# Bilinear samplers of a deformable convolution: samples from plain source tiles, weighted afterwards

## The reference

```python
off1 = conv2d(x, w_off1, b_off1, stride=1, pad=1)          # 18 planes: 9 taps x (dy, dx)
out  = relu(bn_inf(deform_conv(x, off1, w_dc1, 1, 2, 2), g1, beta1, m1, v1))
off2 = conv2d(out, w_off2, b_off2, stride=1, pad=1)
out  = bn_inf(deform_conv(out, off2, w_dc2, 1, 2, 2), g2, beta2, m2, v2)
return relu(out + x)
# deform_conv: for each tap (ky, kx) and each place (y, x) of the output
#   ys = y - 2 + 2*ky + dy ; xs = x - 2 + 2*kx + dx        (pad 2, dilation 2)
#   sampled[i, tap, y, x] = bilinear sample of image channel i at (ys, xs), zero outside
#   out[o, y, x] = sum over i and tap of weight[o, i, tap] * sampled[i, tap, y, x]
```

## Time and profile before

| | |
|---|---|
| median of 3 runs | 812.22 us (811.79 to 814.93) |
| the profiled execution: time, span | 817.21 us, 815.4 us |
| mean granted TensorE clock | 0.840 |
| TensorE matmul / weight load busy | 676.4 us (83%) / 499.2 us (61%), 17818 each |
| VectorE / ScalarE / GpSimd busy | 444.7 us (55%) / 413.7 us (51%) / 132.7 us (16%) |
| DMA | 16.37 MB, of which queue "instruction" 1.98 MB in 121 packets |

### The profile page before, as it was taken

One profiled execution on the slowest core, in us unless ns is written; L12 is line 12 of the kernel. 1 busy time (PEld: TensorE's weight loads), 2 busy tenths in 40 slices (PEclk: granted clock), 3 DMA queues, 4 the chain that ended last, 5 costly groups with the idle time before them and its releaser, 6 DMA issues.

```text
span 815.4 us, 38530 instructions
## 1 busy us (share of the span) xinstructions
PE 676.4 (83%) x17818; PEld 499.2 (61%) x17818; DVE 444.7 (55%) x797; ACT 413.7 (51%) x819; POOL 132.7 (16%) x215
## 2 busy tenths in 40 slices
PE   6788888888858788988778648899999999996556
PEld 1356666666633466665666546688888888874344
DVE  0575555554714555566456482456666666675543
ACT  0667555654414766556455042445666655554512
POOL 7000000000021000000000023324433334420400
PEclk8979797996769798788877665589999999998768
DMA  6400000000002200000000063000000000000002
GB/s 186 86 7 4 5 4 4 4 5 4 5 6 54 37 5 4 4 5 4 5 4 5 4 134 105 2 2 1 0 0 0 0 0 0 0 1 1 1 1 104
DMA packets 7677, 16.37 MB, mean 20 GB/s; under 512 B 1837, under 2 KB 5805, under 8 KB 7141
## 3 DMA queue, kind: packets, MB, share of 16 engines
q1 hardware_dynamic: 7534, 14.21, 7.2%
HBM read 10.34 MB, written 3.87 MB: 17 GB/s over the span
## 4 chain that ended last, share of the span: by engine, by line
PE 75%; issue 9%; ACT 7%; DVE 7%; DMA 1%; POOL 1%; SPq 0%; DVEq 0%; ACTq 0%
PE banks L228 20%; PE banks L145 14%; PE banks L717 8%; PE banks L761 5%; PE banks L694 5%; PE banks L742 4%; PE banks L459 4%; PE banks L776 4%; PE banks L181 2%; ACT hx L274 2%; PE banks L167 2%; PE banks L707 1%; DVE norm_stats L630 1%; ACT y L484 1%; DMA src<-in_x_dram 1%
## 5 line engine op out<-in xcount | busy, mean ns | idle before, releaser
L319 DVE TENSOR_TENSOR s<-hy,hx 128x384 f32<-128x384 f32 (+3 forms) x336 | 144.5, 476 | 147.9 <-PE banks L228 145.9
L228 PE MATMUL banks<-s,y 32*64 32x96 f32 (+9 forms) x10752 | 182.9, 262 | 50.9 <-issue 50.7
L228 PEld LDWEIGHTS banks<-s,y 32*64 32x64 f32 x10752 | 154.6, 149 | 91.2 <-issue 81.5
L145 PE MATMUL banks<-w_dc,tiled 64*64 64x192 f32 x1792 | 121.4, 409 | 13.1 <-issue 7.3
L269 ACT COPY y<-banks 128x384 f32<-128x384 f32 x192 | 80.9, 487 | 95.3 <-PE banks L145 95.3
L145 PEld LDWEIGHTS banks<-w_dc,tiled 64*64 64x64 f32 x1792 | 78.0, 166 | 36.3 <-issue 14.1
L279 ACT ACTIVATE hy<-banks 128x512 f32<-128x512 f32 (+2 forms) x144 | 73.3, 582 | 32.1 <-PE banks L181 31.8
L880 DVE TENSOR_REDUCE stats<-banks 128x16 f32<-128x1024 f32 x32 | 39.2, 1225 | 72.8 <-PE banks L717 72.8
L958 POOL TENSOR_TENSOR y<-y,stats 128x1024 f32<-128x1024 f32 x32 | 60.8, 1901 | 108.2 <-DVE stats L890 108.1
L274 ACT ACTIVATE hx<-banks 128x384 f32<-128x384 f32 x144 | 61.2, 504 | 23.9 <-PE banks L167 19.6
L717 PEld LDWEIGHTS banks<-src,y 64*128 64x128 f32 x1024 | 66.2, 205 | 8.1 <-issue 8.1
(11 more groups left out here) (134 smaller groups left out, 742.5 us busy)
## 6 DMA issues: line engine op xcount, KB each, us to landing
src<-in_x_dram SPq DMA_DIRECT2D x4, 578.0 KB, 5.7
y<-in_w_dram SPq DMA_DIRECT2D x1, 2080.0 KB
off<-in_w_dram SPq DMA_DIRECT2D x2, 1024.0 KB
out_dram<-tokens SPq DMA_DIRECT2D x4, 512.0 KB, 2.6
offsets_dram<-tokens SPq DMA_DIRECT2D x32, 54.0 KB
off<-offsets_dram SPq DMA_DIRECT2D x16, 108.0 KB
w_dc<-in_w_dc_dram SPq DMA_DIRECT2D x2, 288.0 KB, 6.7
y<-in_w_attn_dram SPq DMA_DIRECT2D x1, 512.0 KB, 4.8
```

The costliest lines, as they stand in the source:

```text
L145: last = nc.tensor.matmul(m.ps[C * half:C * half + C, FIRST_BANK + (count + g) % RING, (col % 2) * 192:(col % 2) * 192 + 192], m.tiled[row ...
L228: last = nc.tensor.matmul(out[:, r0:r0 + strip.n, first:first + width], m.y[32 * j:32 * j + 32, g, (s // 3) % 2 * Y_SLOTS + strip.slot, co ...
L319: nc.vector.tensor_tensor(dst, hy, hx[:, :, r0:r0 + strip.n, :], ALU.mult).then_inc(cv.s_ready, 1)
```

## The change

The order of the two products in a sampler is turned round: first plain pixels are sampled, for three kernel columns at once, then the samples are weighted.

- The work is cut into 24 units (4 output rows, ky). A unit has 2 or 3 strips, one for each row of tiles that can reach it: two of 4 rows for ky 0 and 2, one of 4 and two of 2 rows for ky 1, fewer at the image's borders. `sample` makes 32 products per strip; each has 3 x rows x 12 columns (144 or 72) and isn't clipped. Its weights are pixels themselves, from `xt`, the source with pixels on partitions. The banks 0 to 3 hold one unit's samples (3 kernel columns x 4 rows at a pitch of 40).
- At the end of a unit ScalarE takes the samples of two pairs of images, and VectorE those of the other two (`take`, 768 elements each), to `sampled`. The next unit's sampling waits for both.
- When three units have made the 9 taps of 4 rows, `final_pe` weights them: items ("f", row, k) of 9 x 2 x 2 products on 64 x 64 tiles, 128 columns long. ScalarE finishes them (`finish0`, `finish1`). In the second convolution w_dc is scaled by batch norm on VectorE beforehand, and x is added by four products with the identity per item.
- `xt` for the first convolution is laid out on the host and loaded, 2.1 MB, on SP's queue ahead of the loads of w_dc, sel and places. For the second, GpSimd stages the finished rows (`stage_pool`, 4 copies), TensorE turns them (`turn_pe`, items ("t", row), 16 products), and ScalarE copies them to `xt`.
- Coordinates: two items of columns per unit (8 products each, bf16) and one or two of rows (2 products per strip); ScalarE evicts an item of both groups in one activation. The plan puts the items of the unit after next between the groups of 8 sampling products or behind the unit.
- The products of hats for group g = 0 stay on VectorE, those for g = 1 go to GpSimd (`weigh`), one instruction of 12 x rows x 12 elements (576 or 288) per strip and engine. VectorE makes the hats of both groups in one instruction per kind.
- `tiles_pool`, the weighted products and the first weighted items in `offsets_pe` and `offsets_act` go. ScalarE now takes a square root of a loaded row ahead of its first eviction, and for that waits for the loads of the first convolution.

```diff
-IMAGES = [[0, 2, 1, 3], [5, 7, 4, 6]]
+IMAGES = [[0, 2, 4, 6], [1, 3, 5, 7]]
 ROW_COORD, ROW_ONE, ROWS_OFF = 12, 13, 14
-RING, FIRST_BANK = 4, 4
-Y_SLOTS = 5
+FIRST_BANK = 4
+
+UNIT_ROWS = TILE_ROWS
+PLACES = UNIT_ROWS * W
+UNITS = [(row, ky) for row in range(H // UNIT_ROWS) for ky in range(3)]
+PITCH = W + WIN_COLS - TILE_COLS + REACH + 2
+HAT_PITCH = W + 2
+HAT_ROW = 3 * HAT_PITCH
+X_HATS, Y_HATS = 3 * TC * UNIT_ROWS * WIN_COLS, 2 * UNIT_ROWS * HAT_ROW
...
+class Unit:
+    def __init__(self, u, strips_before):
+        self.u = u
+        self.row, self.ky = UNITS[u]
+        self.strips = []
+        for tile_row in range(TR):
+            first = TILE_ROWS * tile_row - 2 * self.ky - UNIT_ROWS * self.row
+            last = min(first + WIN_ROWS, UNIT_ROWS)
+            first = max(first, 0)
+            if last > first:
+                self.strips.append(Strip(tile_row, first, last - first))
+        self.before = strips_before
...
+class Plan:
...
+        self.items = self.units[0].coords + self.units[1].coords
+        self.first = len(self.items)
+        for unit in self.units:
+            row, ky = UNITS[unit.u]
+            todo = self.units[unit.u + 2].coords if unit.u + 2 < len(UNITS) else []
+            final = [("f", row - 1, ky)] if row and ky < 2 else []
+            turn = [("t", row - 2)] if turns and row >= 2 and ky == 2 else []
+            cut = len(todo) if final else (len(todo) + 1) // 2
+            unit.inside, unit.behind = todo[:cut], todo[cut:] + final + turn
+            if unit.u == len(UNITS) - 1:
+                unit.behind = unit.behind + [("f", row, 0), ("f", row, 1)]
+                if turns:
+                    unit.behind = unit.behind + [("t", row - 1), ("t", row)]
+            self.items = self.items + unit.inside + unit.behind
...
-def weighted_pe(nc, pe, m, cv, count, tile_row, part, ky):
...
+def columns_pe(nc, m, cv, bank, u, part):
+
+    row, ky = UNITS[u]
+    kx, n = (0, 2) if part == 0 else (2, 1)
+    for c in range(TC):
         for g in range(2):
             rows = group_rows(g, 1)
+            at = offset_at(row, 3 * ky + kx, 0) + TILE_COLS * c - 2 * kx
+            last = nc.tensor.matmul(
+                ap(m.ps[:, bank + g, c * UNIT_ROWS * WIN_COLS:], [[X_HATS // 3, n], [WIN_COLS, UNIT_ROWS], [1, WIN_COLS]]),
+                m.sel[rows, c, :], ap(m.off_flat[rows, at:], [[HALF_PIX - 2, n], [W, UNIT_ROWS], [1, WIN_COLS]]),
+                start=True, stop=True, skip_group_check=True)
+    last.then_inc(cv.filled, 1)
...
+            last = nc.tensor.matmul(
+                ap(m.ps[:, bank + g, 3 * W * (strip.at % UNIT_ROWS):], [[W, 3], [3 * W, strip.n], [1, W]]),
+                m.sel[rows, strip.tile_row, :], ap(m.off_flat[rows, at:], [[HALF_PIX, 3], [W, strip.n], [1, W]]),
+                start=True, stop=True, skip_group_check=True)
...
+def final_pe(nc, m, cv, bank, row, k):
+
+    for tap in range(TAPS):
+        for p in (k, k + 2):
+            for g in range(2):
+                half = half_of(p, g)
+                rows = slice(C * half, C * half + C)
+                last = nc.tensor.matmul(m.ps[C * g:C * g + C, bank + p // 2, 0:PLACES], cv.w_dc[rows, tap, :],
+                                        m.sampled[rows, row % 2, p, tap, :], start=(tap == 0),
+                                        stop=(tap == TAPS - 1 and cv.k == 0), skip_group_check=True)
+    if cv.k:
+        for p in (k, k + 2):
+            for g in range(2):
+                rows = source_half(m.convs[0], p, g)
+                last = nc.tensor.matmul(
+                    m.ps[C * g:C * g + C, bank + p // 2, 0:PLACES].rearrange("p (r c) -> p r c", c=W),
+                    m.identity[rows, rows], image_rows(m.convs[0].src, p, row)[rows, :, :], start=False, stop=True,
+                    skip_group_check=True)
+    last.then_inc(cv.filled, 1)
...
+def turn_pe(nc, m, bank, tile_row):
+    for c in range(TC):
+        for j in range(PAIRS):
+            last = nc.tensor.matmul(m.ps[32 * j:32 * j + 32, bank, c * P:(c + 1) * P], m.stage[:, tile_row % 2, j, c, :],
+                                    m.identity[:, :], start=True, stop=True, skip_group_check=True)
+    return last
...
+    def sample(unit, strip, c):
+        n = strip.count
+        if c == 0:
+            for g in range(2):
+                pe.wait_ge(cv.s_ready[g], n + 1)
+        for j in range(PAIRS):
+            for g in range(2):
+                half = half_of(j, g)
+                out = m.ps[C * half:C * half + C, j, strip.first * PITCH + TILE_COLS * c + 4:]
+                places = strip.n * WIN_COLS
+                last = nc.tensor.matmul(
+                    ap(out, [[UNIT_ROWS * PITCH - 2, 3], [PITCH, strip.n], [1, WIN_COLS]]),
+                    m.xt[32 * j:32 * j + 32, strip.tile_row, c, C * g:C * g + C],
+                    ap(m.s[32 * j:32 * j + 32, n % SLOTS, g, c * places:], [[TC * places, 3], [WIN_COLS, strip.n], [1, WIN_COLS]]),
+                    start=(strip is unit.strips[0] and c == 0), stop=True, skip_group_check=True)
+        if c == TC - 1:
+            last.then_inc(cv.sampled, 1)
...
+    for unit in cv.plan.units:
+        groups = [(strip, c) for strip in unit.strips for c in range(TC)]
+        if unit.u:
+            for taker in range(2):
+                pe.wait_ge(cv.taken[taker], unit.u)
+        started = 0
+        for k, (strip, c) in enumerate(groups):
+            sample(unit, strip, c)
+            while started < len(unit.inside) and started * len(groups) < len(unit.inside) * k:
+                item_pe(n)
+                n += 1
+                started += 1
+        for _ in unit.inside[started:] + unit.behind:
+            item_pe(n)
+            n += 1
...
+def take(copy, m, cv, unit, j):
+
+    return copy(ap(m.sampled[:, unit.row % 2, j, 3 * unit.ky, :], [[TAPS * PLACES, 2], [W, 3 * UNIT_ROWS], [1, W]]),
+                ap(m.ps[:, j, 4:], [[BANK, 2], [PITCH, 3 * UNIT_ROWS], [1, W]]))
+
+
+def take_waits(engine, cv, unit):
+    engine.wait_ge(cv.sampled, unit.before + len(unit.strips))
+    if unit.row >= 2 and unit.ky == 0:
+        engine.wait_ge(cv.filled, cv.plan.items.index(("f", unit.row - 2, 1)) + 1)
+
+
+def weigh(multiply, engine, m, cv, unit, strip, g):
+
+    n = strip.count
+    if n >= SLOTS:
+        engine.wait_ge(cv.sampled, n - SLOTS + 1)
+    if strip is unit.strips[0]:
+        engine.wait_ge(cv.hats, 2 * unit.u + 2)
+    hy = ap(m.hy[:, unit.u % 2, g, strip.at * HAT_ROW:], [[TILE_COLS, 3 * TC], [HAT_ROW, strip.n], [1, WIN_COLS]])
+    hx = ap(m.hx[:, unit.u % 2, g, strip.first * WIN_COLS:],
+            [[UNIT_ROWS * WIN_COLS, 3 * TC], [WIN_COLS, strip.n], [1, WIN_COLS]])
+    dst = ap(m.s[:, n % SLOTS, g, :], [[strip.n * WIN_COLS, 3 * TC], [WIN_COLS, strip.n], [1, WIN_COLS]])
+    multiply(dst, hy, hx, ALU.mult).then_inc(cv.s_ready[g], 1)
...
+def sampler_pool(nc, pool, m, cv):
+    def stage(tile_row):
+        pool.wait_ge(cv.finished, 2 * tile_row + 2)
+        if tile_row >= 2:
+            pool.wait_ge(cv.filled, cv.plan.items.index(("t", tile_row - 2)) + 1)
+        stage_pool(nc, m, tile_row)
+
+    for unit in cv.plan.units:
+        for strip in unit.strips:
+            weigh(nc.gpsimd.tensor_tensor, pool, m, cv, unit, strip, 1)
+        if cv.k == 0 and unit.row >= 2 and unit.ky == 0:
+            stage(unit.row - 2)
+    if cv.k == 0:
+        stage(TR - 2)
+        stage(TR - 1)
...
+def sampler_dve(nc, dve, m, cv):
+    def hats(unit):
+        dve.wait_ge(cv.emptied, cv.plan.count[unit.coords[1]])
+        hat = m.hx[:, unit.u % 2, :, :]
+        nc.vector.tensor_scalar(hat, hat, 1.0, 1.0, ALU.min, ALU.subtract).then_inc(cv.hats, 1)
+        dve.wait_ge(cv.emptied, cv.plan.count[unit.coords[-1]])
+        hat = m.hy[:, unit.u % 2, :, 0:unit.hat_rows * HAT_ROW]
+        nc.vector.tensor_scalar(hat, hat, 1.0, 1.0, ALU.min, ALU.subtract).then_inc(cv.hats, 1)
+
+    def weights(unit):
+        for strip in unit.strips:
+            weigh(nc.vector.tensor_tensor, dve, m, cv, unit, strip, 0)
+
+    units = cv.plan.units
+    hats(units[0])
+    weights(units[0])
+    hats(units[1])
+    for unit in units:
+        if unit.u + 1 < len(units):
+            weights(units[unit.u + 1])
+        take_waits(dve, cv, unit)
+        take(nc.vector.tensor_copy, m, cv, unit, 2).then_inc(cv.taken[1], 1)
+        if unit.u + 2 < len(units):
+            hats(units[unit.u + 2])
...
-    pe.wait_ge(cv.tiled, TILED // 2)
-    count = 0
-    for kind, f, slot, part in NEAR.first_pairs:
-        weighted_pe(nc, pe, m, cv, count, NEAR.strips[f][slot].tile_row, part, PHASES[f][1])
-        count += 2
...
+            sp.dma_start(m.xt[:, :, :, :], a["xt"]).then_inc(m.xt_loaded, 16)
...
+            for cv in convs:
+                pool.wait_ge(cv.flag_ready, 1)
+                flag = nc.gpsimd.value_load(far_flag[0:1, cv.k:cv.k + 1], min_val=0, max_val=1)
+                with pool.If(flag == 0):
```

(31 more changed lines are left out.)

609 lines of the change are left out of this document (290 added, 319 removed).

## The result

The four executions of the changed kernel had a median of 770.9 us (761.2 to 774.0), beside 812.0 (811.8 to 814.9) for the kernel before. Two of the four, the profiled one (773.97, span 772.1) among them, ran in a slower state of the chip, so the ratio is taken from the other two (761.2 and 768.3) and the control's profile (752.22, span 750.4) is shown beside the first: 0.941 [0.935, 0.948], where the brackets hold the 95% interval. The same kernel timed again later, as a control for the experiments, gave 755.8 (752.1 to 763.1, six executions) against 813.4: 0.930 [0.925, 0.936]. So the change is worth 48 to 57 us by the ratios, where 71 were forecast. Both times lie in the range of 702 to 788; of the likeliest case's own 728 to 757 the first group is 14 us above, and the control just inside.

What follows compares the result with a forecast made beforehand. The samplers were taken to be bound by the number of TensorE's instructions. Terms of 80.8 - 16 + 4.7 + 1.8 = 71.3 us off the profiled 817.2 gave 745.9, or 741 by the median; range 702 to 788.

Steps and rivals of the forecast that it cites:

- likeliest case: Whole kernel: the forecast of 741 us, with a span of 728 to 757 and a chance of 0.58.
- The bound: Both samplers: TensorE's instructions arrive in blocks of 256, one in 4.00 us, so their number sets the time.
- my sign of 15.5: Both samplers: if the forecast is right, about 15.5 ns per TensorE instruction, with samplers of 165 to 172 us.
- Instructions: TensorE in the two samplers: 1240 and 1368 pairs fewer at 31.0 ns, 38.4 + 42.4 = 80.8 us off.
- The interplay of two limits: Samplers: TensorE's own work close under the fetch floor gives back 8 us each (bounds 0 and 20), 16 together.
- Ends: After the samplers: nothing gained behind the first, 1.8 us off behind the second, where only one take is waited for.
- Starts: Before the samplers: without the first weighted products, 2.0 us off in the first convolution and 2.7 in the second.
- Prices beside the path: Per sampler, beside TensorE: ScalarE 99 us, VectorE 98, GpSimd 48 of products, all with cover.
- Rival D: GpSimd's products with runs of 12 elements dearer, strips above 2.24 us: slower, 847 us at 2.7; chance 0.07.
- Rival B: A unit's chain: VectorE and GpSimd exclude each other, takes stop TensorE; 182 us a sampler, 770 in all; chance 0.22.
- Rival C: Samplers: no fetch floor, pauses come with the many short products; 143 us each, 692 in all; chance 0.13.
- The rest: Behind 472 us: nothing changes; a move of 472 to 815 by more than 5 would show the forecast wrong.

Runs made afterwards that it cites:

- the kernels that ran these at 0.93 and 1.00: The changed kernel with no coordinate item behind the take before a turn (753.1 us), and with VectorE's products cut to 12 elements behind 20 strips (762.0 us).

## Why the prediction was nearly right, step by step

*The bound.* Right: a fetch of blocks of 256. Three starts gave me 4.00 us; the median is 3.73 (before) and 3.8 to 3.9 (after). The average of 31.0 ns a pair over the whole sampler hid that: it is 29.3 in the middle and a start that is slower (774 pairs where 30 us hold 1024). Over a whole sampler it came out at 16.4 to 17.2 ns an instruction; my sign of 15.5 was too low even for my own 165 to 172 us, which are 15.8 to 16.9. The control's 171.2 lie in that span, the first profile's 178.3 and 175.4 do not.

*Instructions.* Counts exact. At 29.3 and 29.5 ns the 1240 and 1368 pairs are worth 36.3 and 40.4, 76.7 in place of 80.8.

*The interplay of two limits, 8 us a sampler: the step that failed.* Against the 38.4 and 42.4 of that line, the control lost 11.3 and 13.5, the first profile 18.4 and 17.7: 25 to 36 in all, not 16. Taken apart for the control's first sampler: the middle, 4418 pairs x (30.1 - 29.3) = 3.5 us; the start, 774 - 592 = 182 pairs x 29.3 = 5.3 us; and 2.1 from the unit price above. In the first profile the middle alone is 4374 x (32.0 - 29.3) = 11.8. I had thought only of the middle, and took one granted clock, 0.83 of the earlier trace rows, for the whole sampler. At the start nothing of the fetch was saved: the control's TensorE did 592 pairs in 30 us, busy for 25.25, at 0.50. Its own work at that clock, not the fetch, is the limit in the last 10 us of it, as the three stretches above show: the kernels that ran these at 0.93 and 1.00 did 714 and 712 pairs in the 30 us. What makes the loss in the middle, 3.5 to 11.8 us, stays open: it goes with the granted clock, and no run set that by itself.

*Ends: 1.8 us off, and it came out 4 to 5 longer.* From the end of the second sampler to the first query product it took 27.7 us before, 32.5 and 31.8 after. The sum had no term for leaving the branch. The 2.84 us at 471.95 I had put down to VectorE and ScalarE, as the earlier trace rows names them; the exit of the branch is as long, and was hidden under them, as far as the trace can tell. With VectorE's work gone from there it stayed. The second gap of 3.5 us has no answer in the timeline of before, where all 16 products ran in one piece: I take it that the block behind the exit held them all there, which was not tested. That is 6 us of the miss.

*Starts.* 1.6 and 1.8 us in the first profile, 0.9 and 3.0 in the control, for 2.0 and 2.7: right.

*Prices beside the path.* ScalarE's 99 us a sampler: 97 and 90. VectorE's 98: 124 and 122, for its products took 1287 ns and not 754. GpSimd's 48 us of products: 84 and more. Both have cover, as forecast: 127 operations fill 124 of 171 us. Rival D asked for strips of 2.24 us; they are at 1.86.

*Rival B* gave 770, and the first group's median was 771, but not by its mechanism. Its exclusion is there in full; what it says of the takes is not: in the middle of the control, TensorE waits for a take for under 2 of 133 us. With GpSimd's products taken away, VectorE's fell to 762 ns and the time did not move. So the 770 were met by chance. Only when the instructions shrink further do the takes count. *Rival C* is out by the kernel before with few columns, by the one with split finals and by the pauses that end with the packets.

*The rest* moved by 0.0 in one profile and 9.2 in the other, without a change in its code, so my bound of 5 for it was narrower than the scatter of executions. It also flatters the sum: the control's profile is 65 us below that of before, 6 short of the forecast 71, and 9.2 of the 65 come from this unchanged part.

## What to carry to other kernels

Where TensorE pauses in "issue" at even distances of 256 instructions, count instructions, not columns, and look whether the pauses end with the instruction packets: each pair added cost 26 to 30 ns here. Take the pace from the middle of a stage and price its start by itself, with the granted clock that its own rows show; and when the floor has come down to the height of the next limit, expect little of a single further cut: here instructions returned a third, and columns, GpSimd's share and a wait nothing. Trust no gain of 7 us out of one profile when two executions of one kernel differ by that much.
